# Edge sums of the first message pass: the next batch's softmax steps are issued beside this batch's edge sums

## The reference, cut to what matters

```
xh = (x @ W).reshape(N, H, D)                       # 8 heads of 32
e = leaky_relu(a_src[src] + a_dst[dst], 0.2)        # 50000 edges, sorted by dst
m = segment_max(e, dst);  e = exp(e - m[dst])
denom = segment_sum(e, dst)
out = segment_sum(xh[src] * (e / denom[dst])[:, :, None], dst)
```

## Time and profile before

| | |
|---|---|
| median of 3 runs | 2085.95 us (2084.43 to 2091.15) |
| the profiled execution, its span | 2418.4 us |
| edge phase in it, first own gather to last sums taken | 195.9 to 782 us |
| busy in the whole span: PE, DVE, ACT, POOL | 1368.5, 932.4, 449.9, 1109.8 us |
| second message pass, its gathers | 1563 to 2152 us |

### The profile page before, as it was taken

The page is one execution under the profiler, slowest core; times in us unless marked ns, Lnnn a source line. Parts: engine busy times, 40 slices in busy tenths (PEclk is TensorE's granted clock), DMA queues, the critical chain, the costliest instruction groups (busy, mean ns, idle before and its releaser), DMA issues. The chain is left out here.

```text
span 2418.4 us, 23547 instructions
## 1 busy us (share of the span) xinstructions
PE 1368.5 (57%) x6436; PEld 1105.6 (46%) x6436; DVE 932.4 (39%) x1860; ACT 449.9 (19%) x1265; POOL 1109.8 (46%) x1085
## 2 busy tenths in 40 slices
PE   2512555555546136649999567035463434367988
PEld 1311433444434125549999566013342323245767
DVE  7512433333333387513333123713222222236853
ACT  0111333333334013213333122000000000002320
POOL 4276666666651400463322722173666665631530
PEclk7755667767668565679999778557666767678988
DMA  5463867677665701341111111731333332310002
GB/s 122 118 180 107 270 212 246 229 252 240 223 225 181 195 7 50 111 123 37 62 49 37 61 37 42 178 105 57 94 90 93 90 94 77 94 50 1 0 1 53
DMA packets 155861, 271.60 MB, mean 112 GB/s; under 512 B 23387, under 2 KB 118161, under 8 KB 154625
## 3 DMA queue, kind: packets, MB, share of 16 engines
q0 software_dynamic: 46128, 123.83, 17.2%
q1 hardware_dynamic: 91516, 127.72, 16.6%
q10 hardware_dynamic: 18103, 18.59, 3.4%
HBM read 172.86 MB, written 98.14 MB: 112 GB/s over the span
## 5 line engine op out<-in xcount | busy, mean ns | idle before, releaser
L1119 PE MATMUL bank<-sum_rows,sum_hot 128*125 x896 | 279.6, 469 | 384.5 <-issue 300.9
L1098 POOL DMA_INDIRECT sum_rows<-xn_tab,src_e x392 | 372.6, 951 | 271.0 <-issue 111.3
L739 POOL DMA_INDIRECT gat_rows<-xh_tab,src_e x364 | 349.1, 959 | 196.4 <-issue 103.6
L1119 PEld LDWEIGHTS bank<-sum_rows,sum_hot 128*125 128x125 f32 x896 | 193.9, 231 | 468.0 <-issue 437.4
L811 PE MATMUL bank<-gat_rows,gat_same 128*128 128x264 f32 x784 | 280.5, 500 | 171.8 <-issue 166.6
L811 PEld LDWEIGHTS bank<-gat_rows,gat_same 128*128 128x128 f32 x784 | 179.6, 250 | 218.4 <-issue 178.5
L1145 DVE TENSOR_TENSOR sums<-sums,bank 125x256 f32 x224 | 94.3, 421 | 452.5 <-remote 258.9
L1719 PE MATMUL bank<-weights,e_xthigh 128*128 x896 | 225.1, 334 | 59.2 <-issue 53.8
L855 ACT COPY gat_outs<-bank 128x264 f32<-128x264 f32 x392 | 145.8, 382 | 311.4 <-PE bank L811 231.2
L1719 PEld LDWEIGHTS bank<-weights,e_xthigh 128*128 128x128 f32 x896 | 157.6, 196 | 70.5 <-issue 70.5
L1841 DVE TENSOR_TENSOR e_h<-e_gated,bank 128x342 f32<-128x342 f32 x112 | 57.1, 510 | 335.1 <-ACT e_gated L1789 309.7
(11 more groups left out here) (483 smaller groups left out, 2320.9 us busy)
## 6 DMA issues: line engine op xcount, KB each, us to landing
parts<-gat_outs SPq DMA_DIRECT2D x28, 1904.0 KB
staged<-w_tab SPq DMA_DIRECT2D x8, 2132.0 KB
w_tab<-w_stage SPq DMA_DIRECT2D x16, 682.0 KB
w_raw<-in_L_ffn_w_dram SPq DMA_DIRECT2D x16, 640.0 KB
gat_rows<-xh_tab,src_e POOLq DMA_INDIRECT x392
sum_rows<-xn_tab,src_e POOLq DMA_INDIRECT x392
w_tab<-w_stage SPq DMA_DIRECT2D x8, 768.0 KB
w_raw<-in_L_ffn_w_dram SPq DMA_DIRECT2D x8, 682.0 KB
```

The costliest lines, as they stand in the source:

```text
L739: pool.indirect_dma_start(out=rows[b % R][:, t, :], out_offset=None, in_=k.xh_tab, in_offset=bass.IndirectOffsetOnAxis(ap=k.src_e[:, b * S ...
L1098: pool.indirect_dma_start(out=rows[:, at // IP % (RING * GPAIRS), at % IP, :], out_offset=None, in_=k.xn_tab, in_offset=bass.IndirectOffse ...
L1119: m = nc.tensor.matmul(k.ps[s][0:P, 0:C], hot[u][:, s, c, :], rows[:, bass.ds(slot, 1), c, :].rearrange("p a c -> p (a c)"), start=(c == 0 ...
```

## The change

`find_maxima`, `exps` and `weigh` of a batch no longer stand between two batches of edge sums. PE transposes the masks of b + 1 behind tile 1 of batch b, its logits behind tile 2, its maxima behind tile 7. ACT copies the masks behind tile 0 and runs `exps(b + 1)` behind tile 5. DVE does one batch after another: mark, logits, maxima, weigh. So that the maxima need no output tile, ACT first copies them from PSUM into one of two new tiles, `peaks`, from which DVE subtracts; the copy into the output tile is now made from `peaks` at the batch's start, with its own semaphore, `peaks_out`, for SP. The count of `weights_made` loses its initial 1.

```
-    TURN_AT = 10
+    MASKS_AT, LOGITS_AT, MAXIMA_AT, EXPS_AT = 1, 2, 7, 5
+        peaks = [sb(f"peaks{s}", [EP, SB, H]) for s in range(2)]
...
-                sp.wait_ge(maxima_in, b + 1)
+                sp.wait_ge(peaks_out, b + 1)
...
-                v.tensor_tensor(shifted[:, :, :], logit[:, :, :], turned_max[b % 2]..., ALU.subtract)
+                v.tensor_tensor(shifted[:, :, :], logit[:, :, :], peaks[b % 2][:, :, :], ALU.subtract)
...
-            mark(0)
-            sum_logits(0)
             for b in range(NB):
+                mark(b)
+                sum_logits(b)
                 find_maxima(b)
-                if b < NB - 1:
-                    mark(b + 1)
                 weigh(b)
-                if b < NB - 1:
-                    sum_logits(b + 1)
...
         @block.tensor
...
+                    if t == MASKS_AT and ahead:
+                        turn_masks(b + 1)
+                    if t == LOGITS_AT and ahead:
+                        turn_logits(b + 1)
+                    if t == MAXIMA_AT and ahead:
+                        turn_maxima(b + 1)
...
         @block.scalar
...
-                act.wait_ge(outs_free, b + 1)
                 act.wait_ge(maxima_turned, b + 1)
-                nc.scalar.copy(outs[b % 2][:, :, C + H:RW], turned_max[b % 2]...).then_inc(maxima_in, 1)
+                nc.scalar.copy(peaks[b % 2][:, :, :], turned_max[b % 2]...).then_inc(maxima_in, 1)
...
+            exps(0)
             for b in range(NB):
-                exps(b)
+                act.wait_ge(outs_free, b + 1)
+                nc.scalar.copy(outs[b % 2][:, :, C + H:RW], peaks[b % 2][:, :, :]).then_inc(peaks_out, 1)
...
-                    if t == SB // 2 and b < NB - 1:
+                    if t == 0 and ahead:
                         keep_masks(b + 1)
+                    if t == EXPS_AT and ahead:
+                        exps(b + 1)
```

More of the change, by code:

```diff
@@ L707, in edge_phase @@
         weights_made, messages, sums, taken = sem("weights_made"), sem("messages"), sem("sums"), sem("taken")
+        peaks_out = sem("peaks_out")
         w, banks = k.turned, k.ps[6:7]
@@ L768, in find_maxima @@
                 dve.wait_ge(maxima_in, b + 1)
-                v.tensor_tensor(shifted[:, :, :], logit[:, :, :], turned_max[b % 2].rearrange("p (t h) -> p t h", h=H), ALU.subtract).then_inc(less_max, 1)
+                v.tensor_tensor(shifted[:, :, :], logit[:, :, :], peaks[b % 2][:, :, :], ALU.subtract).then_inc(less_max, 1)
             def weigh(b):
-                dve.wait_ge(weights_made, b + 2)
+                dve.wait_ge(weights_made, b + 1)
                 for half in range(2):
@@ L819, in _ @@
             for b in range(NB):
+                ahead = b < NB - 1
                 pe.wait_ge(same_made, b + 1)
[L821 to L827, removed]
+                for t in range(SB):
+                    if t % (SB // 2) == 0:
+                        pe.wait_ge(messages, 2 * b + 1 + t // (SB // 2))
+                    add_edges(b, t)
+                    if t == MASKS_AT and ahead:
                         turn_masks(b + 1)
-                if b < NB - 1:
-                    turn_maxima(b + 1)
+                    if t == LOGITS_AT and ahead:
+                        turn_logits(b + 1)
+                    if t == MAXIMA_AT and ahead:
+                        turn_maxima(b + 1)
         @block.scalar
@@ L834, in _ @@
             act.sem_inc(taken, BK)
-            act.sem_inc(weights_made, 1)
             def keep_masks(b):
@@ L841, in exps @@
             def exps(b):
-                act.wait_ge(outs_free, b + 1)
                 act.wait_ge(maxima_turned, b + 1)
-                nc.scalar.copy(outs[b % 2][:, :, C + H:RW], turned_max[b % 2].rearrange("p (t h) -> p t h", h=H)).then_inc(maxima_in, 1)
+                nc.scalar.copy(peaks[b % 2][:, :, :], turned_max[b % 2].rearrange("p (t h) -> p t h", h=H)).then_inc(maxima_in, 1)
                 act.wait_ge(less_max, b + 1)
```

## The result

The changed kernel takes 2085.52 us (median of 20 runs, 2080.12 to 2092.87), the kernel before 2080.93 us beside it (20 runs, 2074.09 to 2091.15): 4.6 us more, ratio 1.0025 [1.0013, 1.0037]. The forecast was 2085.0 with 1 us less. The size is near nothing, but this first comparison stands on the slower side, against the forecast.

What follows compares the result with a forecast made beforehand. The prediction took POOL's gathers to bound the edge stage in the timed runs, so the hidden idle start gains nothing; +2 us of tail and -3 us of gather waits gave -1, forecast 2085 us, range 2030 to 2094.

Steps and rivals of the forecast that it cites:

- If PE's stalls beside the gathers belong to profiling, the timed runs lack them.: Edge, expert and second gather stages: profiling stalls make up 270 to 308 of the 332 us between profile and timed runs.
- Rival (a): Edge stage: part of PE's stalls is real in timed runs; 35 us less, 2051 (2026 to 2079); chance 0.28.
- PE's 166.6 us that waited "for nothing that the profile shows": Edge stage: waits of PE's edge matmuls without a visible cause in the profile before, 166.6 us.
- POOL's pace is real.: Edge stage, timed runs: POOL needs 1.265 us per gather, 17.7 us per batch of 14, 460.4 us for all 364.
- the floor case: Edge stage: POOL's gathers set the end, the hidden idle start gains nothing; forecast 2085, range 2079 to 2093, chance 0.50.
- Rival (b): Edge stage: all stalls are real and the profile stands; 95 us less, 1991; chance 0.11.
- The landing, "the same in both kernels": After POOL's last gather: its rows land in an estimated 2 us, bounds 0 and 17.7, no difference between kernels.
- The tail behind the landing, +2 with bounds -2 and +8.: After the last gather: work of 14.3 to 15.6 us before, 13.6 to 22.6 after; taken as +2 us.
- rival (c): Edge stage: PE, broken up by waits, stays cold; 18.9 us a batch, about 25 us slower, 2111; chance 0.10.
- The -3 for gathers that wait.: Edge stage, timed runs: a few gathers wait before; 3 of the 87.2 us come back, bounds 0 and 87.2.
- The sum.: Whole kernel: +2 for the tail and -3 for waiting gathers give -1 us, forecast 2085.
- The port.: Edge stage: the subtraction's two SBUF operands could put up to 7.6 us on POOL by the rule; by the rows, nothing.

Runs made afterwards that it cites:

- `hold_after_2`: Changed kernel, with SP holding back batch 25's output tile and weights until the last batch's rows are in, on a fast chip (about 2082 us): 2079.49 us, ratio 0.9999.
- `late_all`: Changed kernel with masks, logits, maxima and exponentials back at their old places in every batch, DVE's new order and `peaks` kept: 2078.84 us, ratio 0.9986.
- the second: The changed kernel run again, unedited, against the kernel before on a fast chip: 2083.36 us, ratio 1.0001 [0.9982, 1.0020].

## Why the prediction was right or wrong

**"If PE's stalls beside the gathers belong to profiling, the timed runs lack them."** The conclusion for the timed runs held, the reason was wrong. On the chips of 2082 us profiled and timed executions agree (2089.9 within 2075.14 to 2091.64 of the same kernel), and so they do on the chip of 2415 us (2425.4 for a median of 2429.87). The 332 us lie between two chips, not between a profiled and a timed execution. The chip of the profile of before isn't known, but its 2418.4 us lie within the 2390.01 to 2432.72 timed on the slow one, and its stage starts at 195.9 us, as there (196.8) and not as on a fast one (181.6). The split over stages, which the prediction added up, was that of a slow chip. Its sign for the profile after, about 2325, is refuted on either: 2081.2 and 2425.4. Rival (a), part of the stalls real in the timed runs, fails on the fast chips with POOL's 2.7 us of waits.

**PE's 166.6 us that waited "for nothing that the profile shows".** I took them for the stall. On a fast chip the same line has 137.7 of them, so most are the idle start of the batches, whose releaser the trace doesn't name.

**"POOL's pace is real."** This held: 17.6 us a batch in both orders, waits of 2.7 us before and 1.2 after; less gathering gave 45 us with the old order and 99 with the new. The idle start that was hidden lay beside POOL's gathers, as the floor case said.

**Rival (b), the profile as it stands.** On the slow chip its condition is met, as with POOL's waits of 87.2 us. It forecast 95 us less; the change costs about 15 there. So even with real stalls the idle start was not what could be had. With the new order POOL's waits are 110.9 us (103.2, and 7.7 that are remote) and not fewer than 87.2. The trace suggests one way: a stalled PE now holds DVE's maxima, DVE's weighing and ACT's copies within the same batch. That the new places are the cause, and not DVE's order, was not tried on that chip and stays open.

**The landing, "the same in both kernels".** This is the step that failed in the sum. The estimate was 2 us for both. It is 4.1 us before and 6.8 to 7.1 after, because batch 25's output tile and weights now go out beside the last gathers; held back, the landing was 2.9. I had noted that SP issues the same DMAs in the same order, and that 11 edges now wait for a gather, and had not put the two together: what these edges finish is sent later too. `hold_after_2` shows this cause and `late_all` agrees (2.7 us).

**The tail behind the landing, +2 with bounds -2 and +8.** It measured +0.7. TensorE was cold as the new tail began and warm at its end, as the bounds assumed; two windows of after:

```profile
645.00:655.00 10.00, 5.41 (x15) 4.15 (x16) 1.40 (x4) 1.59 (x5) 0.00 (x0) 0.50 0.47 162
655.00:665.00 10.00, 9.90 (x47) 7.69 (x45) 4.23 (x3) 8.78 (x27) 0.00 (x0) 1.00 0.49 167
```

PE had been idle for 5.18 us when it took up the edges at 649.59. The granted clock is 0.50 (1.2 GHz) in the first window and 1.00 in the next; in the kernel before it is also 0.50 for its last batch's first five microseconds. The copies of the sums follow each other at 0.88 us in the one and at 6.15 / 14 = 0.44 us in the other. The Trainium skill's "TensorE: Matmul & The Clock Gate", in its table on why this matters, asks for matmuls without idle gaps; the trace agrees that an edge costs twice as much at the lower level. Over the stage the clock is the same, 0.76 against 0.77, so rival (c) is refuted.

**The -3 for gathers that wait.** There were 2.7 us of such waits on a fast chip; 1.5 of them went.

**The sum.** -1 was forecast; the traces show +3.4 (+2.7 landing, +0.7 behind it) at the last copy and +4.8 at the next phase's first transfer; the wait for batch 26's output tile was in no term. The landing is what turns the sum to the slower side. The first comparison measured +4.6, the second +0.2 (0.9982 to 1.0020), the kernel before against itself -3.0. The longer tail is there in both profiles of the changed kernel (23.5 and 23.7 us against 20.1, and 17.8 with the third batch gathered ahead). That the time of the whole rises by it is plausible and not shown. Two things warn against reading one from the other: the two profiled executions of the changed kernel span 2081.2 and 2091.3 us and both reach the next phase's first gather at 675.2, so those 10 us arise later; and the kernel with the third batch ahead has the short tail and a median 5.1 us above the kernel before.

**The port.** The rule of the Trainium skill's "SBUF — State Buffer" (section on the two separate sides) would have put up to 7.6 us on POOL. The gathers' median is 957 ns in both kernels and their longest 1038 ns after and 1043 before: no effect here.

## What to carry to other kernels

Before a long profile is explained by the profiler, compare it with another execution on the same chip: here a gap of 332 us was the chip's. Where one engine issues without a pause but its own, the idle time of the others isn't a loss, and work hidden in it gives nothing; take away part of that engine's work in an experiment and see whether the order is worth anything then (54 us here). An engine's idle time without a named releaser need not be a stall: compare it with a run in which the suspected cause is absent. When a wait moves forward in a queue, the outputs of what stands behind it are sent later: ask what these transfers now run beside, above all at the end of a stage, where the last gather is on the path.

## What the runs showed of the hardware that was not expected

- The same kernel takes 2082 us on two chips and 2415 on a third. In the edge stage the difference goes with the number of gathers: 479 against 586 us with 14 a batch (the latter 195.9 to 782.2), 431.7 against 431.1 with 7. The other stages, where nothing was taken away, stay slow: with 7 gathers the whole still takes 2260 against 2038 us. POOL's gather is as fast on either (957 ns). What stalls PE beside dense gathers on that chip stays open.
- On the fast chips a gather of 128 rows lands 2.7 to 8.8 us after its issue; the last one took 4 us longer with an output tile of 1904 KB and weights sent beside it.
- On a fast chip the unchanged kernel spreads over 2074 to 2093 us.
